# Variances of the decayed attention in the bank of its state products, and neighbourhood attention joined to the mixture of experts in one program region

## The chip, the cores and the metric

The kernel runs on one core of one Trainium2 chip. The metric is the device time of one execution in microseconds (us), the median of several runs. Engines: PE is TensorE (PEld its weight loads), ACT ScalarE, DVE VectorE, POOL GpSimd, SP the engine that issues most DMAs.

## The reference

A small language-model tower on 32 sequences of 512 tokens with 64 features: spectral token features, then two layers, each an attention and a feed-forward part, each of them preceded by a layer norm and followed by a residual sum.

```
x = tok(x)                                   # FFT features, MLP
x = x + neighbourhood_attn(layernorm(x))     # 8 heads, 31 neighbours, dilation 2
t = layernorm(x)
p = softmax(t @ router_w.T); top 2 of 8 experts, weights renormalised to sum 1
x = x + t + sum_e w_e * (gelu(t @ w1[e] + b1[e]) @ w2[e] + b2[e])
x = x + decayed_attn(layernorm(x))           # causal, scores scaled by 0.99^(q-k)
x = x + soft_moe(layernorm(x))               # routed softly by token position, 8 experts
```

Every layer norm needs, per token, 1/sqrt(variance + eps), spread over that token's 64 features.

## The kernel before

Activations stay in SBUF as 16 rows (`s.h`, `s.z`), each 128 partitions x 512 tokens, two sequences of 64 features one above the other. Each stage is one function that opens its own `nc.Block()`: a region in which every engine has its own hand-written instruction list, in order, joined to the others by semaphores alone. A region ends with a meeting of all engines. `unrolled(count, unroll, (lead, stage), ...)` writes the list of an engine: in loop step n it calls each stage for item n + lead, in the order in which the stages stand. So the order of an engine's queue is this list of stages, and a wait in it holds everything behind it on that engine.

**Layer norm.** When a row of `s.h` is final, POOL squares it (`square`, L488, into `s.sq[p % 8]`). For every four rows PE sums the squares over features into one PSUM bank (`variance`, L495), ACT takes Ln and Exp(-0.5 x) into `s.rstd`, SP writes that to DRAM (`hop`, L507) and reads it back spread over partitions (`spread`, L519, two DMAs per row), and POOL multiplies (`scaled`, L535). `keep_warm` (L502) issues bf16 products whose results nobody reads.

**Neighbourhood attention** (`neighbourhood_attention`, L902 to L1348). At its end PE makes the router's logits of the first four rows (L1153, L1160). DVE ranks them: nine instructions (`first_ranked`, L1309 to L1318) before the residual of the last row (L1295), and the rest (`next_ranked`, L1322 to L1341) after it. ACT gives the weights by an Exp of the gap (L1256) and computes the last norm (`deviations_of(LAST)`, L1244 and L1246) from the last variance, which PE makes between two groups of `keep_warm` (L1166 to L1168).

**Mixture of experts** (`mixture_of_experts`, L1387). 16 rows times 4 pairs of experts are 64 steps. Step n: PE `first(n)` (L1533, 4 products into two of three banks), ACT `gelu(n)` (L1604, two instructions), PE `expand(n)` (L1547, the route weights), DVE `weigh(n)` (L1735), PE `second(n)` (L1563). PE and ACT run `first` and `gelu` nine steps ahead of the loop up to step 42 (`AHEAD_G`, `LAST_AHEAD`), four ahead after it, `expand` and `weigh` three, `second` two. `first(n)` waits for the first half of `gelu(n-1)`. PE `turn` (L1523) turns the route weights and ACT copies them twice (L1618, L1622) before `expand(0)`. The router of the next four rows runs 24 steps ahead on PE, ACT and DVE. In step 33 ACT computes a norm with Ln and Exp (L1633, L1635). Between Gelu and these it loads other function tables. The region begins on ACT with a table load (L1582), and PE's first wait is for credits that ACT gives behind it.

**Decayed attention** (`decayed_attention`, L1760). Per row PE runs `scores` (L1886, then the state products L1892 into the bank `p_w`), `project` of the next row (L1871, L1876), and `outputs` (L1905, L1909, into the bank `p_y`). `project(n)` needs a copy of row n with its two halves exchanged, which SP fetches (`fetch_swapped`, L1355, two DMAs). SP's list per loop step n is `fetch(n+2)`, `former(n)` (the hop and spreads of the norm that feeds this stage) and `after(n)` (`normal(n-5)`, hop and spreads of the next norm). Variances go into `p_y`: `former` in step 0 and `after` in steps 5, 9 and 13 stand ahead of `outputs`, which waits until ACT has made the reciprocal deviations:

```
if at.n == 0:
    te.wait_ge(s.n_rstd, quad(2, LAST))
if at.n >= 5:
    te.wait_ge(s.n_rstd, quad(3, (at.n - 5) // 4))
unrolled(NP, 2, (0, scores), (1, project), (0, former), (0, after), (0, outputs))
```

Of the kernel before, what the change touches and what calls it, by code (L numbers as in the profile page):

```python
# [31 lines left out]
NP = NB // 2  # L32
# [869 lines left out]
def neighbourhood_attention(nc, s, v, r):  # L902

    with ExitStack() as ctx:
# [6 lines left out]
        def sem(name):  # L911
            return ctx.enter_context(nc.semaphore("na_" + name))
# [16 lines left out]
        logits_t = row(s.z, NP)  # L929
        logits, best, masked, picked, weights = [s.z[:, NP + 1 + k // 2, 256 * (k % 2):256 * (k % 2) + 256].rearrange("p (g e) -> p g e", e=NE) for k in range(5)]  # L930
        first_of, second_of, top, gap, w_best, w_next = [s.z[:, NP + 3, 256 + ROUTED * k:256 + ROUTED * k + ROUTED] for k in range(6)]
        p_route = p_s[1][:, 0].rearrange("p h a w -> p (h a w)")
        s_zero, s_rl, s_lt, s_rt, s_link, s_gap, s_less, s_next = [sem(x) for x in ("zero", "rl", "lt", "rt", "link", "gap", "less", "next")]
        p_first = p_t[:, 0:4, :].rearrange("p g c -> p (g c)")
        block = ctx.enter_context(nc.Block())

        @block.gpsimd
        def _(pool):
            nc.gpsimd.memset(r.ct_in[:], 0.0).then_inc(s_zero, 1)
# [76 lines left out]
        def _(te):  # L1016
# [139 lines left out]
            def first_logits_turned(at):  # L1156
                if at.n == TURNS - 1:
                    te.wait_ge(s_lt, 1)
                    for tile in range(4):
                        mm = nc.tensor.transpose(p_route[:, tile * 128:tile * 128 + 128], logits_t[:, tile * 128:tile * 128 + 128], const(s, "ident"))  # L1160
                    mm.then_inc(s_rt, 1)
# [4 lines left out]
            keep_warm(nc, s, p_o[:], 5)  # L1166
            variance_of(LAST)
            keep_warm(nc, s, p_o[:], 4)  # L1168

        @block.scalar  # L1170
        def _(sc):
# [64 lines left out]
            def fetch_first_logits(at):  # L1236
                if at.n == TURNS - 1:
                    sc.wait_ge(s_rl, 1)
                    nc.scalar.activation(logits_t, p_route, ACT.Copy).then_inc(s_lt, 1)
# [15 lines left out]
            sc.wait_ge(s_gap, 1)  # L1255
            nc.scalar.activation(gap, gap, ACT.Exp, scale=-1.0).then_inc(s_less, 1)  # L1256
            deviations_of(LAST)

        @block.vector
        def _(ve):  # L1260
# [37 lines left out]
            links = [0]  # L1298

            def linked(ins):  # L1300

                ins.then_inc(s_link, 1)
                links[0] += 1
                ve.wait_ge(s_link, links[0])

            def first_ranked():
                v = nc.vector
                ve.wait_ge(s_rt, 1)
                linked(v.tensor_copy(logits.rearrange("p (g b) e -> p g (b e)", b=2),  # L1309
                                     p_route.rearrange("p (g n) -> p g n", n=32)[:, :, 0:2 * NE]))  # L1310
                linked(v.tensor_reduce(first_of, logits, AX, ALU.max))
                linked(v.tensor_tensor(best, logits, over_experts(first_of), ALU.is_equal))
                linked(v.tensor_tensor(best, best, rank_of(s), ALU.mult))
                linked(v.tensor_reduce(top, best, AX, ALU.max))
                linked(v.tensor_tensor(best, best, over_experts(top), ALU.is_equal))
                linked(v.scalar_tensor_tensor(out=masked, in0=best, scalar=-3.0e38, in1=logits, op0=ALU.mult, op1=ALU.add))
                linked(v.tensor_reduce(second_of, masked, AX, ALU.max))
                v.tensor_tensor(gap, first_of, second_of, ALU.subtract).then_inc(s_gap, 1)  # L1318

            def next_ranked():  # L1320
                v = nc.vector
                linked(v.tensor_tensor(picked, masked, over_experts(second_of), ALU.is_equal))  # L1322
                linked(v.tensor_tensor(picked, picked, rank_of(s), ALU.mult))
                linked(v.tensor_reduce(top, picked, AX, ALU.max))
                linked(v.tensor_tensor(picked, picked, over_experts(top), ALU.is_equal))
                ve.wait_ge(s_less, 1)
                linked(v.tensor_scalar(top, gap, 1.0, None, ALU.add))
                linked(v.reciprocal(w_best, top))
                v.tensor_tensor(w_next, gap, w_best, ALU.mult).then_inc(s_next, 1)
                linked(v.tensor_tensor(best, best, over_experts(w_best), ALU.mult))  # L1330
                ve.wait_ge(s_next, 1)
                linked(v.tensor_tensor(picked, picked, over_experts(w_next), ALU.mult))
                linked(v.tensor_tensor(weights, best, picked, ALU.add))
                linked(v.tensor_copy(r.high[:], weights))
                ve.wait_ge(s_zero, 1)
                linked(v.tensor_tensor(weights, weights, r.high[:], ALU.subtract))
                v.tensor_copy(parts_of(r)[:, :, :, :, 0:NE], by_place(r.high[:]))
                linked(v.tensor_copy(r.middle[:], weights))
                v.tensor_copy(parts_of(r)[:, :, :, :, NE:2 * NE], by_place(r.middle[:]))
# [47 lines left out]
def mixture_of_experts(nc, s, r):  # L1387
# [3 lines left out]
    with ExitStack() as ctx:  # L1391
# [45 lines left out]
        def _(pool):  # L1437
# [919 lines left out]
```

## Time and profile before

| | before |
|---|---|
| median of 3 runs | 876.51 us (876.44 to 878.71) |
| profiled execution | 880.86 us, of it span 879.1 us |
| mean granted PE clock | 0.976 |
| busy PE | 804.4 us (92%) |
| busy DVE | 583.7 us (66%) |
| busy ACT | 476.7 us (54%) |
| busy POOL | 301.2 us (34%) |
| neighbourhood attention | to about 379 us |
| mixture of experts | 379 to 559 us |
| decayed attention | 559 to 671 us |

The sum of the engines' busy time is larger than the span because they work at once. Where PE is near its full share, a wait of another engine costs nothing; where PE waits, what it waits for sets the time.

### The profile page before, as it was taken

How to read it: one execution, taken by the hardware profiler on the slowest of the kernel's cores; microseconds unless marked ns; L12 is line 12 of the kernel's file. 1: busy time of each engine (PE TensorE's matmuls, PEld its weight loads, DVE VectorE, ACT ScalarE, POOL GpSimd, SP SyncE). 2: the span in 40 equal slices, each digit the busy share in tenths (PEclk: the TensorE clock that was granted, in tenths of full speed). 3: DMA queues.
4: the chain of work that ended last, by engine and by line, in shares of the span. 5: the costliest groups of instructions: out<-in, count | busy, mean ns of one | idle time of the engine just before them, and what ended most of it. 6: DMA issues, size and time to landing. Idle time of an engine off the chain costs nothing. (4 is left out here: it accounts for less than half of the span.)

```text
span 879.1 us, 28915 instructions
## 1 busy us (share of the span) xinstructions
PE 804.4 (92%) x12642; PEld 410.5 (47%) x12648; DVE 583.7 (66%) x854; ACT 476.7 (54%) x656; POOL 301.2 (34%) x292
## 2 busy tenths in 40 slices
PE   3989799999999999679999799799998899999996
PEld 2232377776776776413333233376663333333332
DVE  5547477777776776637777955477673377777776
ACT  2254377778778777346565656412221455555553
POOL 3235453633534423202443454473453710000000
PEclk9999799999999999979999999999999999999998
DMA  4210221002001001020000220053321011111111
GB/s 108 27 30 1 85 73 31 4 5 63 4 4 64 4 4 65 1 61 1 1 2 1 83 63 1 18 164 98 95 83 41 13 33 44 47 49 49 49 50 37
DMA packets 38670, 36.38 MB, mean 41 GB/s; under 512 B 20817, under 2 KB 25074, under 8 KB 38418
## 3 DMA queue, kind: packets, MB, share of 16 engines
q1 hardware_dynamic: 37474, 32.52, 13.1%
q8 instruction: 101, 1.65, 0.8%
q10 hardware_dynamic: 1072, 2.02, 0.7%
q14 instruction: 23, 0.19, 0.1%
HBM read 18.79 MB, written 7.34 MB: 30 GB/s over the span
## 5 line engine op out<-in xcount | busy, mean ns | idle before, releaser
L2233 ACT ACTIVATE se_a<-se_p,cols 128x512 f32<-128x512 f32 x128 | 92.8, 775 | 75.9 <-PE se_p L2186 75.9
L2253 DVE SCALAR_TENSOR_TENSOR se_a<-se_p,cols,z 128x1024 f32<-128x1024 f32 x64 | 82.2, 1284 | 48.8 <-PE se_p L2196 48.8
L1273 DVE TENSOR_REDUCE na_rowmax<-na_ps 128x16 f32<-128x1024 f32 x64 | 78.1, 1220 | 54.0 <-PE na_ps L1111 54.0
L1604 ACT ACTIVATE z<-me_p,cols 128x512 f32<-128x512 f32 x128 | 81.1, 685 | 59.4 <-PE me_p L1533 54.6
L1735 DVE TENSOR_TENSOR me_gw<-me_pc,z 128x1024 f32<-128x1024 f32 x64 | 78.3, 1223 | 46.7 <-PE me_pc L1547 38.3
L947 POOL TENSOR_TENSOR z<-na_k,const 128x512 f32<-128x512 f32 x62 | 62.5, 1040 | 129.6 <-ACT na_k L1192 129.6
L488 POOL TENSOR_TENSOR n_sq<-h 128x512 f32<-128x512 f32 x64 | 68.4, 1074 | 94.6 <-DVE h L858 40.0
L1563 PE MATMUL me_py<-me_gw,w_out 64*64 64x512 f32 x512 | 88.8, 601 | 0.0
L1533 PE MATMUL me_p<-z,moe_w 64*64 64x512 f32 x512 | 82.8, 621 | 6.4 <-issue 3.8
L535 POOL TENSOR_TENSOR z<-h,n_bc 128x512 f32<-128x512 f32 x58 | 75.1, 1306 | 25.7 <-DMA n_bc<-n_spread 25.6
L1276 DVE TENSOR_TENSOR z<-na_ps,na_rowmax 128x1024 f32<-128x1024 f32 x64 | 78.4, 1225 | 2.2
L1120 PE MATMUL na_pt<-const,z 128*128 128x128 f32 x512 | 70.0, 280 | 5.4 <-ACT z L1219 3.1
L1219 ACT ACTIVATE z<-z 128x1024 f32<-128x1024 f32 x64 | 67.4, 1053 | 8.1 <-DVE z L1276 7.4
L2186 PE MATMUL se_p<-z,f_w 64*64 64x512 f32 x512 | 68.8, 603 | 1.9 <-ACTq L548 1.1
L2196 PE MATMUL se_p<-se_a,f_w 64*64 64x512 f32 x512 | 68.3, 599 | 1.3 <-DVE se_a L2253 1.3
L1226 ACT ACTIVATE na_et<-na_pt 128x1024 f32<-128x1024 f32 x64 | 65.4, 1021 | 7.4 <-PE na_pt L1120 6.5
L2208 PE MATMUL se_py<-se_a,w_out 64*64 64x512 f32 x512 | 67.3, 589 | 0.5 <-DVE se_a L2253 0.5
L1120 PEld LDWEIGHTS na_pt<-const,z 128*128 128x128 f32 x512 | 56.7, 141 | 20.9 <-issue 15.3
L1454 POOL TENSOR_TENSOR h<-h,me_even 128x512 f32<-128x512 f32 x15 | 20.1, 1340 | 96.2 <-DVE me_even L1750 96.2
L1134 PEld LDWEIGHTS na_po<-na_v,na_et 128*32 128x32 f32 x4096 | 41.8, 110 | 21.8 <-ACT na_et L1226 11.4
L1111 PE MATMUL na_ps<-z,na_q 32*32 32x256 f32 x2048 | 51.6, 390 | 0.2
L1213 ACT ACTIVATE na_v<-na_pm 64x512 f32<-64x512 f32 x64 | 38.6, 602 | 21.3 <-PE na_pm L1066 20.9
(359 smaller groups left out, 1290.2 us busy)
## 6 DMA issues: line engine op xcount, KB each, us to landing
n_bc<-n_spread SPq DMA_DIRECT2D x116, 128.0 KB, 3.1
z<-z SPq DMA_DIRECT2D x64, 128.0 KB, 2.4
out<-se_rows SPq DMA_DIRECT2D x16, 256.0 KB, 2.1
n_spread<-n_rstd SPq DMA_DIRECT2D x12, 256.0 KB, 2.0
const<-in_const ACTq DMA_DIRECT2D x1, 1114.0 KB, 8.2
const<-in_const ACTq DMA_DIRECT2D x1, 562.0 KB, 4.2
f_w<-in_L_ffn_W SPq DMA_DIRECT2D x4, 128.0 KB
const<-in_const ACTq DMA_DIRECT2D x1, 258.0 KB, 3.0
```

The costliest lines, as they stand in the source:

```text
L488: return nc.gpsimd.tensor_tensor(s.sq[p % 8][:], row(s.h, p), row(s.h, p), ALU.mult)
L535: return eng.tensor_tensor(row(s.z, p), row(s.h, p), s.bc[p % 4][:], ALU.mult)
L1120: mm = nc.tensor.transpose(p_t[:, c, :], e[b][:, 2 * c:2 * c + 2, :].rearrange("p h w -> p (h w)"), const(s, "ident"))
L1273: nc.vector.tensor_reduce(rowmax[b][:], scored, AX, ALU.max).then_inc(s_max, 1)
L1276: nc.vector.tensor_tensor(e[b], scored, rowmax[b][:].unsqueeze(2).broadcast_to([128, GROUPS, WIN]), ALU.subtract).then_inc(s_diff, 1)
L1533: mm = nc.tensor.matmul(hidden(at.n, b)[half[e2], :], s.moe_w1[half[b], 2 * ep + e2, :], row(s.z, at.of(4))[half[b], :], start=True, stop= ...
L1563: mm = nc.tensor.matmul(p_y[half[b], e2, :], s.moe_w2[half[e2], ep, :], gw[at.k % 2][half[e2], b, :], start=(ep == 0 and b != e2), stop=(e ...
L1604: nc.scalar.activation(g[at.n % 7][:, b, :], hidden(at.n, b)[:], ACT.Gelu, bias=col(s, "moe_b1", ep)).then_inc(s_g, 1)
L1735: nc.vector.tensor_tensor(gw[at.k % 2][:], p_c[:], g[at.n % 7], ALU.mult).then_inc(s_gw, 1)
L2186: mm = nc.tensor.matmul(hidden(at.n, e2)[half[b], :], s.f1_w1[half[e2], 2 * ep + e2, :], z[half[e2], :], start=True, stop=True, skip_group ...
L2233: nc.scalar.activation(a1[at.k % 2][:, e2, :], hidden(at.n, e2)[:], ACT.Relu, scale=col(s, "f1_g1", 2 * ep + e2), bias=col(s, "f1_be1", 2 ...
L2253: nc.vector.scalar_tensor_tensor(out=a2[at.k % 2][:], in0=p_2[:], scalar=col(s, "f1_be2", ep), in1=s.f1_w[:, ep, :].unsqueeze(1).broadcast ...
```

## The change

Two parts. **One region:** attention and mixture share one block, so no meeting of the engines and no second block entry lies between them. Attention's tail loses the last variance, both groups of `keep_warm`, the last norm, and the ranking from its fifth instruction on. The ranking is completed at the head of DVE's mixture list (`rank_on`, 21 instructions), with Tanh instead of Exp for the weights; ACT does the Tanh behind `gelu(2)`. The last variance goes into a mixture bank behind `first(4)`, ACT copies it behind `gelu(4)`, and takes Ln and Exp at the end of step 8. `keep_warm` now has two products behind each of `first(0)` to `first(5)`. `gelu(6)` waits for the complete ranking, since its buffer holds the ranking's numbers. `turn(0)` and its two copies move one step back. POOL multiplies the last four rows by that norm in rows 2 and 3, two each, not one each in rows 0 to 3. **Decayed attention:** variances go into `p_w`, behind `outputs`; the next state products wait for ACT's Ln (`n_ln`), which has then read the bank.

```diff
@@ neighbourhood_attention
-            keep_warm(nc, s, p_o[:], 5)
-            variance_of(LAST)
-            keep_warm(nc, s, p_o[:], 4)
...
-            sc.wait_ge(s_gap, 1)
-            nc.scalar.activation(gap, gap, ACT.Exp, scale=-1.0).then_inc(s_less, 1)
-            deviations_of(LAST)
...
-            next_ranked()
@@ mixture_of_experts, POOL
-                if p < 4:
-                    rescale(1, 4 * LAST + p)
+                if 2 <= p < 4:
+                    rescale(1, 4 * LAST + 2 * (p - 2))
+                    rescale(1, 4 * LAST + 2 * (p - 2) + 1)
@@ mixture_of_experts, PE
                     if c == 1:
-                        te.wait_ge(s_route, linked_to(0, 1))
+                        te.wait_ge(r.s_h, done(NP - 1))
...
                 mm.then_inc(s_w1, 1)
-                if at.n < 2:
-                    keep_warm(nc, s, p_c[:, 0, :], 3)
+                if at.n < 6:
+                    keep_warm(nc, s, p_c[:, 1, :], 2)
+                if at.n == 4:
+                    te.wait_ge(s.n_sq, nth(1, NP - 1))
+                    variance(nc, s, LAST, p_y[:, 1, :]).then_inc(s.n_var, 1)
...
+                if at.n == 0:
+                    te.wait_ge(s_last, 1)
@@ mixture_of_experts, ACT
+                if at.n == 6:
+                    sc.wait_ge(s_ctin, done(0))
                 for b in range(2):
                     nc.scalar.activation(g[at.n % 7][:, b, :], hidden(at.n, b)[:], ACT.Gelu, bias=col(s, "moe_b1", ep)).then_inc(s_g, 1)
+                if at.n == 2:
+                    sc.wait_ge(s_gap, done(0))
+                    nc.scalar.activation(r.gap, r.gap, ACT.Tanh, scale=0.5).then_inc(s_tanh, 1)
+                if at.n == 4:
+                    sc.wait_ge(s.n_var, quad(1, LAST))
+                    nc.scalar.activation(s.rstd[:, LAST, :], p_y[:, 1, :], ACT.Copy).then_inc(s_last, 1)
+
+            def last_deviations(at):
+                if at.n == 8:
+                    sc.wait_ge(s_last, 1)
+                    nc.scalar.activation(s.rstd[:, LAST, :], s.rstd[:, LAST, :], ACT.Ln, bias=s.eps[:]).then_inc(s.n_ln, 1)
+                    sc.wait_ge(s.n_ln, 2 + LAST)
+                    nc.scalar.activation(s.rstd[:, LAST, :], s.rstd[:, LAST, :], ACT.Exp, scale=-0.5).then_inc(s.n_rstd, 1)
@@ decayed_attention, PE
+                if at.n == 1:
+                    te.wait_ge(s.n_ln, 7)
+                if at.n >= 6 and at.n % 4 == 2:
+                    te.wait_ge(s.n_ln, 8 + (at.n - 6) // 4)
...
-                if at.n == 0:
-                    te.wait_ge(s.n_rstd, quad(2, LAST))
-                if at.n >= 5:
-                    te.wait_ge(s.n_rstd, quad(3, (at.n - 5) // 4))
...
-                te.wait_ge(s_h, done(last))
+                te.wait_ge(s_st, done(last))
                 te.wait_ge(s.n_sq, nth(3, 4 * n + 3))
-                variance(nc, s, n, p_y).then_inc(s.n_var, 1)
+                variance(nc, s, n, p_w).then_inc(s.n_var, 1)
...
-            unrolled(NP, 2, (0, scores), (1, project), (0, former), (0, after), (0, outputs))
+            unrolled(NP, 2, (0, scores), (1, project), (0, outputs), (0, former), (0, after))
@@ build
-                neighbourhood_attention(nc, s, v, r)
-            mixture_of_experts(nc, s, r)
+                block = inner.enter_context(nc.Block())
+                neighbourhood_attention(nc, s, v, r, inner, block)
+            mixture_of_experts(nc, s, r, inner, block)
```

**ACT, steps 7 to 9 of the mixture.** Before: the copy of the router's logits (`me_logits_t`) stands between the Gelu pairs of `gelu(17)` and `gelu(18)`; `me_odd` is a copy of a finished row's sum.

```order
261 L1604 ACTIVATE z<-me_p,cols 128x512 x6
262 L1594 ACTIVATE me_logits_t<-me_pr 128x512
263 L1604 ACTIVATE z<-me_p,cols 128x512 x2
264 L1612 ACTIVATE me_odd<-me_py 128x512
265 L1604 ACTIVATE z<-me_p,cols 128x512 x4
```

The same place with the change:

```order
260 L1590 ACTIVATE z<-me_p,cols 128x512 x6
261 L1578 ACTIVATE me_logits_t<-me_pr 128x512
262 L1601 ACT_TABLE_LOAD
263 L1601 ACTIVATE n_rstd<-n_rstd,eps 128x512
264 L1603 ACT_TABLE_LOAD
265 L1603 ACTIVATE n_rstd<-n_rstd 128x512
266 L1590 ACT_TABLE_LOAD
267 L1590 ACTIVATE z<-me_p,cols 128x512 x2
268 L1611 ACTIVATE me_odd<-me_py 128x512
```

Three table loads, Ln and Exp now stand ahead of `gelu(18)`.

**PE, beginning of the decayed attention.** `da_pqk` and `da_pv` are `project`, `da_ps` and `da_pw` `scores`, `da_py` `outputs`, and L495 the variance. Before:

```order
603 L1886 MATMUL da_ps<-da_q,da_k 128x128 x8
604 L1892 MATMUL da_pw<-da_v,da_kd 64x64 x6
605 L1871 MATMUL da_pqk<-z,w_in 64x512 x4
606 L1876 MATMUL da_pv<-w_out,z 128x128 x8
607 L495 MATMUL da_py<-n_sq,const 32x512 x4
608 L1905 MATMUL da_py<-da_sm,da_v 64x128 x8
609 L1909 MATMUL da_py<-da_qd,da_state 128x128 x3
610 L1886 MATMUL da_ps<-da_q,da_k 128x128 x8
```

With the change:

```order
606 L1925 MATMUL da_ps<-da_q,da_k 128x128 x8
607 L1935 MATMUL da_pw<-da_v,da_kd 64x64 x6
608 L1910 MATMUL da_pqk<-z,w_in 64x512 x4
609 L1915 MATMUL da_pv<-w_out,z 128x128 x8
610 L1944 MATMUL da_py<-da_sm,da_v 64x128 x8
611 L1948 MATMUL da_py<-da_qd,da_state 128x128 x3
612 L495 MATMUL da_pw<-n_sq,const 32x512 x4
613 L1925 MATMUL da_ps<-da_q,da_k 128x128 x8
```

The variance moved behind both groups of `outputs` and into the bank `da_pw`; the steps 5, 9 and 13 change in the same way.

## Rows read from the trace of the kernel before

**Rows 1.** Windows: stretch, its us, busy us by engine, granted PE clock, DMA.

```profile
368.00:380.00 12.00, 5.43 (x18) 1.16 (x18) 10.28 (x24) 2.41 (x4) 3.37 (x3) 0.85 0.06 23
380.00:388.00 8.00, 7.60 (x34) 1.57 (x38) 0.00 (x0) 3.02 (x6) 1.26 (x1) 0.59 0.52 133
505.00:510.00 5.00, 4.48 (x32) 1.42 (x36) 2.63 (x6) 0.77 (x2) 0.00 (x0) 0.66 0.23 81
570.00:576.00 6.00, 5.65 (x58) 4.53 (x58) 1.69 (x2) 0.20 (x1) 0.27 (x1) 0.72 0.47 171
```

**Rows 2.** Timeline, attention to mixture: start, length, engine, line, work, idle before.

```profile
367.09 0.60 ACT L1234 ACTIVATE z<-na_pm 128x512 f32<-128x512 f32 x1 [3.58 <-PE na_pm L1078]
...
367.74 1.13 PE L1088 MATMUL na_pm<-z,w_out 128*128 128x512 f32 x2 [0.69 <-ACT z L1234]
...
371.06 0.74 DVE L1295 SCALAR_TENSOR_TENSOR h<-na_pm,cols,h 128x512 f32<-128x512 f32 x1
...
378.37 0.49 DVE L1341 TENSOR_TENSOR me_ctin<-z,me_middle 128x128 f32<-128x128 f32 x2
379.14 1.28 ACT L1582 ACT_TABLE_LOAD   x1 [2.70 <-PEq L904]
...
380.40 1.99 PE L1533 MATMUL me_p<-z,moe_w 64*64 64x512 f32 x8 [3.77 <-issue]
```

**Rows 3.** Timeline, opening of the mixture: `weigh(0)`.

```profile
396.80 1.23 DVE L1735 TENSOR_TENSOR me_gw<-me_pc,z 128x1024 f32<-128x1024 f32 x1 [5.03 <-PE me_pc L1547]
```

**Rows 4.** Timeline, DVE cast in step 8 and the product behind it.

```profile
421.09 1.35 DVE L1719 CAST me_ctin<-me_high 128x256 f32<-128x256 bf16 x1
...
423.83 0.41 PE L1547 MATMUL me_pc<-me_ct_parts,pick_b 64*64 64x512 bf16 x4 [1.89 <-DVE me_gw L1735]
```

**Rows 5.** Timeline, mixture steps 9 and 10: `gelu(18)` and `first(19)`.

```profile
427.18 1.27 ACT L1604 ACTIVATE z<-me_p,cols 128x512 f32<-128x512 f32 x2 [0.42 <-PE me_p L1533]
...
428.71 1.09 PE L1533 MATMUL me_p<-z,moe_w 64*64 64x512 f32 x8
```

**Rows 6.** Timeline of ACT, mixture step 33: loads, with the Ln of two tiles.

```profile
489.69 1.28 ACT L1633 ACT_TABLE_LOAD   x1
490.99 1.15 ACT L1633 ACTIVATE n_rstd<-n_rstd,eps 128x1024 f32<-128x1024 f32 x1
492.21 1.28 ACT L1635 ACT_TABLE_LOAD   x1
```

**Rows 7.** Timeline, PE behind a wait inside the mixture.

```profile
505.52 0.41 PE L1547 MATMUL me_pc<-me_ct_parts,pick_b 64*64 64x512 bf16 x4 [2.95 <-DVE me_gw L1735]
```

**Rows 8.** Waits, decayed attention: total us, times, longest.

```profile
PE da_py L1905 <- ACT n_rstd L1957: 4.7, 3, 1.6
...
PE da_py L1905 <- ACT n_rstd L1942: 2.7, 1, 2.7
```

**Rows 9.** Timeline, `fetch(3)` and `project(3)` of the decayed attention.

```profile
574.75 1.18 SPq L1355 DMA_DIRECT2D z<-z  x2
...
580.97 1.09 PE L1871 MATMUL da_pqk<-z,w_in 64*64 64x512 f32 x8
```

**Rows 10.** Swapped-row DMAs of 560 to 600 us, issue to landing.

```profile
DMA to landing us min/median/max: 2.2/2.6/3.6
```

**Rows 11.** Timeline, step 5 of the decayed attention up to `project(8)`.

```profile
600.99 0.69 ACT L1955 ACTIVATE n_rstd<-da_py,eps 128x512 f32<-128x512 f32 x1 [0.82 <-PE da_py L495]
601.71 0.63 ACT L1957 ACTIVATE n_rstd<-n_rstd 128x512 f32<-128x512 f32 x1
...
602.48 1.09 PE L1905 MATMUL da_py<-da_sm,da_v 128*64 128x128 f32 x16 [1.56 <-ACT n_rstd L1957]
603.50 0.94 PE L1909 MATMUL da_py<-da_qd,da_state 128*128 128x128 f32 x6
...
605.59 1.18 SPq L1355 DMA_DIRECT2D z<-z  x2
...
611.55 1.09 PE L1871 MATMUL da_pqk<-z,w_in 64*64 64x512 f32 x8
```

More of the change, by code:

```diff
@@ L928, in neighbourhood_attention @@
         s_first, s_near = sem("s_first"), sem("near")
[L929 to L933, printed above, removed]
+        p_route = p_s[1][:, 1].rearrange("p h a w -> p (h a w)")
+        s_rl, s_lt, s_rt = [sem(x) for x in ("rl", "lt", "rt")]
         p_first = p_t[:, 0:4, :].rearrange("p g c -> p (g c)")
-        block = ctx.enter_context(nc.Block())
+        r.s_h = s_h
         @block.gpsimd
         def _(pool):
-            nc.gpsimd.memset(r.ct_in[:], 0.0).then_inc(s_zero, 1)
+            nc.gpsimd.memset(r.ct_in[:], 0.0).then_inc(r.s_zero, 1)
             give_credits(pool, s_blk)
@@ L1317, in first_ranked @@
[L1317 to L1339, printed above, removed]
-                for b in range(2):
-                    v.tensor_tensor(parts_of(r)[:, :, b, :, 2 * NE:3 * NE], by_place(weights)[:, :, b], by_place(r.middle[:])[:, :, b], ALU.subtract)
@@ L1360, with route_buffers, chained, linked @@
 LINKS = 21
-def route_buffers(nc, ctx):
+def route_buffers(nc, s, ctx):
     r = Buffers()
     r.ct_in = ctx.enter_context(nc.sbuf_tensor("me_ctin", [128, 4, 2, 2, 2, ROUTES], F32))
+    r.logits_t = row(s.z, NB - 2)
+    r.logits, r.best, r.masked, r.picked, r.weights = [row(s.z, n)[:, c:c + 256].rearrange("p (g e) -> p g e", e=NE)
+                                                       for n, c in ((NB - 1, 0), (NB - 1, 256), (NB - 4, 0), (NB - 4, 256), (NB - 3, 0))]
+    r.first_of, r.second_of, r.top, r.gap, r.w_best, r.w_next = [row(s.z, NB - 3)[:, 256 + ROUTED * k:256 + ROUTED * k + ROUTED] for k in range(6)]
+    r.s_zero, r.s_link = [ctx.enter_context(nc.semaphore("r_" + x)) for x in ("zero", "link")]
+    r.links = 0
     r.high, r.middle = [ctx.enter_context(nc.sbuf_tensor("me_" + x, [128, ROUTED, NE], BF16)) for x in ("high", "middle")]
     return r
+def chained(ve, r):
+    def linked(ins):
+        ins.then_inc(r.s_link, 1)
+        r.links += 1
+        ve.wait_ge(r.s_link, r.links)
+    return linked
 def over_experts(x):
@@ L1576, in spreads @@
                     variance(nc, s, n, p_r).then_inc(s.n_var, 1)
-            unrolled(EP * NP, 16, (4, turn), (AHEAD_G, while_ahead(first)), (BEHIND_G, when_behind(first)), (3, expand), (2, second), (AHEAD, logits_of), (0, spreads))
+            unrolled(EP * NP, 16, (4, turn), (AHEAD_G, while_ahead(first)), (BEHIND_G, when_behind(first)), (3, first_turn), (3, expand), (2, second), (AHEAD, logits_of), (0, spreads))
         @block.scalar
@@ L1583, in _ @@
             give_credits(sc, s_ct, s_parts, s_g, s_copied, s_odd)
-            for x in (s_lt, s_tanh):
-                sc.sem_inc(x, done(0))
+            give_credits(sc, s_tanh)
+            sc.sem_inc(s_lt, done(0))
             def router(at):
@@ L1635, in deviations @@
                         nc.scalar.activation(s.rstd[:, 0:2, :], s.rstd[:, 0:2, :], ACT.Exp, scale=-0.5).then_inc(s.n_rstd, 2)
-            unrolled(EP * NP, 16, (4, fetch), (AHEAD_G, while_ahead(gelu)), (BEHIND_G, when_behind(gelu)), (2, fetch_odd), (4, fetch_whole), (AHEAD, router), (0, deviations))
+            unrolled(EP * NP, 16, (4, fetch), (AHEAD_G, while_ahead(gelu)), (BEHIND_G, when_behind(gelu)), (3, first_fetch), (2, fetch_odd), (4, fetch_whole), (AHEAD, router),
+                     (0, deviations), (0, last_deviations))
         @block.vector
@@ L1954, in deviations @@
                 sc.wait_ge(s.n_z, nth(2, NP - 1))
[L1955 removed]
+                nc.scalar.activation(s.rstd[:, n, :], p_w[:], ACT.Ln, bias=s.eps[:]).then_inc(s.n_ln, 1)
                 sc.wait_ge(s.n_ln, 8 + n)
```

126 lines of the change are left out of this document (79 added, 47 removed).

## The prediction

> **What bounds the kernel now.** I read the busy shares first: PE is busy 92% of the span, so only what delays PE counts. The windows come next, because they show the few places where PE does not run full [rows 1]. From 368 to 380 us PE is busy 5.4 of 12 us while DVE is busy 10.3: the ranking of the first four rows bounds the end of the attention. From 380 to 388 us PE is granted 0.59 of full speed, a mixture of the levels 1.2 and 2.4 GHz, which costs 8 x 0.41 = 3.3 us. The timeline then names the steps between the regions [rows 2]: ACT's last attention copy ends at 367.69, PE's at 368.87, DVE's ranking at 378.86; the table load starts 0.28 later and PE's first mixture product at 380.40, as that load ends. In the decayed attention the waits show PE standing for the reciprocal deviations, once 2.7 us and three times together 4.7 us [rows 8].
>
> **Term 1, one region.** Nothing now holds ACT behind DVE. It can branch and load its table 0.28 us behind its last copy: 367.97 to 369.25. `first(0)` starts at 369.2, 11.2 us earlier than 380.40. The steps up to `first(6)` go at the pace of `first` (1.09), half a Gelu pair (0.64) and two hand-overs of 0.1, so 1.9 us [rows 5]; six of them are 11.4 us. Router logits, their transposes and the moved variance do not quite fit in the gaps; I charge 1.8. `first(6)` starts at 382.4. Its 1.1, the Gelu pair 1.3, the first route copy 0.6 (as the 0.60 of rows 2), `expand(0)` 0.4 [rows 4] and hand-overs 0.2 bring `weigh(0)` to 386.0, where it was 396.80 [rows 3]: **-10.8 us**. In this the slow-clock loss of 3.3 us is gone, because PE no longer stands from 376 to 380 us, and the turn and copy that used to be early now stand on the path.
>
> Is DVE in time? Before, 17 instructions took 371.80 to 378.86, 0.42 us each [rows 2]. Five fewer stand ahead of the last residual, so it moves from 371.06 to about 369.0 and ends at 369.8. Nine instructions lead to the Tanh wait, reached at 373.5. Tanh comes behind `gelu(2)`, which ends near 376.3. Twelve instructions more end at 381.7. `gelu(6)` wants them at 383.6, so 1.9 us of cover remain.
>
> The two removed groups of `keep_warm`, the removed variance and ACT's Exp of the gap were beside DVE's chain and count nothing by themselves. The new `keep_warm` pairs stand in the gap in which PE waits for Gelu and are covered too. The squares and the hop come later than before, but the four rows scaled by them are first needed by the router in step 24, more than 30 us behind step 8.
>
> **Term 2, POOL.** In step 8 a DVE cast takes 1.35 us beside a POOL product, and PE waits 1.89 us [rows 4]. POOL's scaling in row 1 is moved away. Bounds: 0 if the square still collides, -1.35 at most. I take **-1.0**, since the POOL row that leaves is the one beside the cast.
>
> **Term 3, table loads inside the mixture.** ACT now executes, between `gelu(17)` and `gelu(18)`, three loads, an Ln and an Exp. Durations: 1.28 each [rows 6], Ln 0.69 and Exp 0.63 of one tile [rows 11]; with gaps of 0.02 to 0.07 [rows 6] this is 5.2 us. ACT was idle 0.42 there [rows 5], so `gelu(18)` is 4.8 us late. Being nine steps ahead does not help: `first(19)` waits for its first half and stands on PE in front of `expand(13)` and `second(12)`. First half done at 427.18 + 4.8 + 0.64 = 432.6, `first(19)` at 432.8 where it was 428.71: 4.1 us. Behind a wait of 2.95 us [rows 7] PE ran at 0.66 from 505 to 510 us [rows 1], which costs 5 x 0.34 = 1.7 us; this wait is longer, so I add it. **+5.8 us**, and PE has no slack afterwards to take it back.
>
> Here the Trainium skill has two rules. ScalarE: Activation LUTs (What ACT_TABLE_LOAD costs) puts every switch at 1.28 us plus a drain of about 1.38 us. In rows 6 the load is followed by its function in 0.02 us and preceded by 0.07 us, so the trace does not show the drain; with it the term would be about 4.1 us larger. The same page (Table sets) says that Ln followed by Exp needs one load, as one set holds both. The trace shows a load ahead of each [rows 6], and the change's list for ACT has the same; with one load fewer the term would be 1.3 us smaller. I go by the rows.
>
> **Term 4, start of the decayed attention.** `outputs(0)` now goes ahead of the variance: 1.09 + 0.94 = 2.0 us [rows 11], less 0.1 for overlap, so the variance, the deviations, the hop and all that SP has behind them come 1.9 us later. PE itself saves the 2.7 us wait. But SP's `fetch(3)` stands behind the hop. It was issued at 574.75, its second half 0.6 later [rows 9], and lands 2.6 us behind that [rows 10], at 577.9; now at 579.8. `project(3)` was at 580.97 [rows 9] and cannot start before 579.8: -1.1 us. Without that limit it would be wanted at about 577.2, so PE stands about 2.6 us. The same stand before led to a clock of 0.72 from 570 to 576 us [rows 1], 6 x 0.28 = 1.7 us. That loss lay ahead of 580.97 and is in the old time; now it would come again behind it. **+0.6 us** with it, -1.1 without. The new wait for `n_ln` before the state products costs 0.3 us here, inside PE's slack against SP.
>
> **Term 5, steps 5, 9 and 13.** Each loses its wait, 4.7 us together [rows 8]. ACT's Ln (0.69) now runs beside `scores`, which is longer, so the new wait is hidden. What is late next is SP again: variance 1.95 us later, so `fetch(8)`, issued at 605.59 [rows 11], lands at 605.59 + 0.6 + 2.6 + 1.95 = 610.7, while `project(8)`, at 611.55 before, is wanted 1.56 earlier, at 610.0. That gives 0.7 us back in step 5 and in step 9; behind step 13 no row is fetched. Bounds: -4.7 with nothing given back, 0 if the DMAs take everything. **-3.3 us.**
>
> **Sum.** -10.8 - 1.0 + 5.8 + 0.6 - 3.3 = -8.7 us. Against the profiled execution of 880.86 us (span 879.1 and 1.76 around it) this is 872.2. The median of the runs is 876.51, 4.35 below the profiled one; with the same difference I predict **867.8 us**.
>
> **Rivals.**
> - *The clock holds* through the waits of terms 3 and 4. For it: behind the 1.56 us wait of step 5 PE ran at once at its full pace, 1.09 us for L1905 [rows 11]. Against: the windows behind the 2.95 us and the 2.7 us wait [rows 1], which these waits equal or exceed. -8.7 - 3.4 = -12.1: 864.4 us. Chance 0.17.
> - *The opening runs at half speed* as it did from 380 to 388, since PE is lightly used before it. Against: it is no longer empty for 4 us. Up to 3.3 us come back: 871.1 us. Chance 0.12.
> - *The ranking is late.* POOL and DVE collide as in rows 4, the cover of 1.9 us is used up, and `gelu(6)` waits. The point: DVE instructions at 0.6 us each in place of 0.42. At 0.9 us it costs 4 us: 871.8 us. Chance 0.06. The change would then not do what it says, as the ranking still bounds the opening.
> - *One load fewer*, the rule of the page named above: 1.3 us less, 866.5 us. Both lists speak against it. Chance 0.02.
> - *The drain of 1.4 us per switch*, the page's other rule: 871.9 us. Chance 0.02.
> - *Slower: the fetches of swapped rows become the bound.* SP issues them behind a hop that is now 1.95 us later, in steps 0, 5 and 9, among the spreads' traffic. If each lands x later than 2.6 us, and each stall slows the clock (1.7 more in steps 5 and 9), the price is 3x + 3.4. It cancels the gain at x = 1.8, a landing of 4.4 us; at x = 3 the time is 867.8 + 12.4 = 880.2 us. Against: the slowest landing was 3.6 us [rows 10]. Chance 0.05.
>
> **The numbers.** The forecast has the remaining 0.56. The low end takes the held clock and half of what term 5 gives back; the high end takes the slow opening or the drain and a term 5 near zero: 862.0 to 873.5 us. A change of 0.3% (2.6 us) is about what a measurement of this kernel can tell from none. Only the last rival, and half a dozen small misses together, come near it: faster 0.92, same 0.04, slower 0.04.
>
> **What would show it.** In the new trace: PE's first mixture product within 0.5 us of the end of ACT's load near 369 us; `weigh(0)` near 386; three table loads behind the router's logits copy of step 8 with a PE wait near 4 us and a clock below 1; PE waiting for a swapped row before `project(3)`; 0.5 to 1 us before `project(8)` and `project(12)`; no PE wait for the reciprocal deviations. The forecast is wrong if the opening does not start before 371 us, or if the wait in step 10 is below 2 us.

## The result

The change runs at 873.0 us (median of 20 runs, 867.88 to 878.58), the kernel before at 877.02 us (median of 20, 872.83 to 879.55). The ratio is 0.9956, 95% interval 0.9938 to 0.9973: faster by 4.0 us, where 8.7 were forecast. The profiled execution of the change took 872.89 us (span 871.2, mean granted clock 0.980) against 880.86 for the kernel before (0.976). This one pair says -8.0 us, close to the forecast; the runs say half of it. What follows looks for the 4.7 us between the forecast and the runs.

First the handover from attention to mixture, in the timeline of the change:

```profile
366.37 0.60 ACT L1228 ACTIVATE z<-na_pm 128x512 f32<-128x512 f32 x1 [3.68 <-PE na_pm L1075]
366.99 1.28 ACT L1566 ACT_TABLE_LOAD   x1
...
367.02 1.12 PE L1085 MATMUL na_pm<-z,w_out 128*128 128x512 f32 x2 [0.69 <-ACT z L1228]
368.08 1.09 PE L1512 MATMUL me_p<-z,moe_w 64*64 64x512 f32 x8
...
378.51 0.49 DVE L1681 TENSOR_TENSOR me_ctin<-z,me_middle 128x128 f32<-128x128 f32 x2
...
384.35 1.23 DVE L1773 TENSOR_TENSOR me_gw<-me_pc,z 128x1024 f32<-128x1024 f32 x1 [2.95 <-PE me_pc L1529]
```

Against [rows 2, 3] the load directly follows ACT's last copy, and `first(0)` starts 1.06 us behind the start of PE's last attention product where it was 12.66. It starts as that product ends, 0.19 us before ACT's load does, so the load is not on PE's path here. It runs at full pace: 1.09 us, where it took 1.99. DVE's ranking (to 379.00) is no longer ahead of anything: `gelu(6)`, the first to want its result, starts at 382.02. From that last product (L1085, L1088 before) to `weigh(0)` it is 17.33 us, before 29.06.

Step 8 of the mixture, ACT and then PE:

```profile
413.17 1.28 ACT L1601 ACT_TABLE_LOAD   x1
414.46 0.72 ACT L1601 ACTIVATE n_rstd<-n_rstd,eps 128x512 f32<-128x512 f32 x1
415.20 1.28 ACT L1603 ACT_TABLE_LOAD   x1
416.50 0.63 ACT L1603 ACTIVATE n_rstd<-n_rstd 128x512 f32<-128x512 f32 x1
417.14 1.28 ACT L1590 ACT_TABLE_LOAD   x1
...
419.18 1.99 PE L1512 MATMUL me_p<-z,moe_w 64*64 64x512 f32 x8 [4.01 <-ACT z L1590]
```

The three loads are there, each followed by its function in 0.01 or 0.02 us, and `first(19)` waits 4.01 us and then takes 1.99 instead of 1.09 us. A little earlier stands the cast of [rows 4], now with no POOL product beside it:

```profile
408.55 0.28 DVE L1757 CAST me_ctin<-me_high 128x256 f32<-128x256 bf16 x1
...
410.22 0.41 PE L1529 MATMUL me_pc<-me_ct_parts,pick_b 64*64 64x512 bf16 x4 [0.81 <-DVE me_gw L1773]
```

The cast takes 0.28 us where it took 1.35, and PE waits 0.81 where it waited 1.89.

The decayed attention, from the waits of TensorE there, and the timeline of its swapped rows:

```profile
PE da_pqk L1910 <- DMA z<-z: 6.0, 3, 3.3
...
PE da_pw L1935 <- ACT n_rstd L1980: 0.4, 1, 0.4
```

```profile
567.22 3.10 SPq L519 DMA_DIRECT2D n_bc<-n_spread  x4
570.42 1.18 SPq L1310 DMA_DIRECT2D z<-z  x2
...
573.66 1.67 PE L1910 MATMUL da_pqk<-z,w_in 64*64 64x512 f32 x8 [3.35 <-DMA z<-z]
...
600.52 1.97 SPq L519 DMA_DIRECT2D n_bc<-n_spread  x2
602.59 1.18 SPq L1310 DMA_DIRECT2D z<-z  x2
...
605.96 1.09 PE L1910 MATMUL da_pqk<-z,w_in 64*64 64x512 f32 x8 [1.72 <-DMA z<-z]
...
630.33 1.09 PE L1910 MATMUL da_pqk<-z,w_in 64*64 64x512 f32 x8 [0.94 <-DMA z<-z]
```

The 7.4 us of waits for the reciprocal deviations [rows 8] are gone. In their place stand 6.0 us of waits for swapped rows (`project(3)`, `project(8)`, `project(12)`) and 0.4 for `n_ln`. One kind of wait was exchanged for another. The spreads (L519) that SP issues ahead of these fetches also take longer to issue than in the kernel before, where they are

```profile
572.26 2.39 SPq L519 DMA_DIRECT2D n_bc<-n_spread  x4
...
604.38 1.11 SPq L519 DMA_DIRECT2D n_bc<-n_spread  x2
```

### The profile page after: what moved, and what is told of

Its sections match the earlier page's. It is cut to its first block and busy times, and to the rows that moved or that the text cites. A ratio compares the mean times of both kernels' runs of the same rounds, so it can differ in the third digit from the quotient of the medians.

```text
span 871.2 us, 28909 instructions
## 1 busy us (share of the span) xinstructions
PE 799.5 (92%) x12638; PEld 408.3 (47%) x12645; DVE 584.0 (67%) x853; ACT 480.8 (55%) x660; POOL 301.2 (35%) x292
## 5 line engine op out<-in xcount | busy, mean ns | idle before, releaser
L1590 ACT ACTIVATE z<-me_p,cols 128x512 f32<-128x512 f32 x128 | 81.1, 685 | 59.1 <-PE me_p L1512 54.3
L1117 PEld LDWEIGHTS na_pt<-const,z 128*128 128x128 f32 x512 | 56.4, 141 | 20.8 <-issue 15.3
```

Of the source, the lines that this page charges most:

```text
L1117: mm = nc.tensor.transpose(p_t[:, c, :], e[b][:, 2 * c:2 * c + 2, :].rearrange("p h w -> p (h w)"), const(s, "ident"))
L1590: nc.scalar.activation(g[at.n % 7][:, b, :], hidden(at.n, b)[:], ACT.Gelu, bias=col(s, "moe_b1", ep)).then_inc(s_g, 1)
```

## The experiments

Two pieces of the change were run alone, then two of its suspected costs were taken away.

**The region alone.** The change with the decayed attention of before:

```diff
-            unrolled(NP, 2, (0, scores), (1, project), (0, outputs), (0, former), (0, after))
+            unrolled(NP, 2, (0, scores), (1, project), (0, former), (0, after), (0, outputs))
...
-                variance(nc, s, n, p_w).then_inc(s.n_var, 1)
+                variance(nc, s, n, p_y).then_inc(s.n_var, 1)
```

> The change with the decayed attention of before: one program region, the variance of the last four rows behind first(4), the ranking in the mixture, and nothing else. Theory (profiles read event by event): the pair of profiles gave first(0) 12.3 us earlier, the pair in step 8 another 1.15, the three table loads +6.4, so that the decayed attention starts 6.9 us earlier; the decayed part's own net was -1 us. So the profiled execution of this kernel should start its decayed attention near 553.4 us and end 1 us later than that of the change, and its median should lie 1 us above the change's 873.0, near 874, ratio to before near 0.9965. Rival (the decayed part is the whole of the gain that the medians show, the region gives back in clock and loads what it saves): ratio 1.000, median near 877.

Measured: 874.53 us, ratio 0.9972 (0.9948 to 0.9996). Its decayed attention started at 555.00 us, not near 553.4, and its profiled execution ended 1.6 us above that of the change instead of 1. The median came where the first theory had it, and the rival's 1.000 lies just outside the interval: the region is most of the gain.

**The decayed attention alone.** The kernel before with the change's variances, the same edit in the other direction.

> The kernel before with the decayed attention of the change: variances in the bank of the states' products, behind the outputs. The two program regions stay. Theory: the outputs no longer wait for the deviations (4.7 us at three steps before), but the fetch of the swapped row stands behind the later hop, and project(3), project(8), project(12) wait for it by 3.35, 1.72 and 0.94 us (a sum of 6.0) as in the change: net -1 us, median near 876, ratio 0.9985 to 1.000. Rival (all of the gain of the medians comes from here): ratio 0.9956, median near 873. Rival (the waits for the fetch cost more where the clock falls): ratio 1.002.

Measured: 879.17 us, ratio 1.0028 (1.0005 to 1.0051): no gain, rather a loss. The waits are as expected, 5.4 us for swapped rows in place of 7.4 for the deviations:

```profile
PE da_pqk L1871 <- DMA z<-z: 5.4, 3, 3.5
```

The rival in which the decayed attention is the gain is out, and so is the theory's 0.9985 to 1.000; nearest is the rival with 1.002, the waits for the fetch costing more where the clock falls. But by its profile the part itself is not longer (109.6 us, table below). What is longer is the span behind the first product of the last mixture: 192.6 us against 190.9 in that of the kernel before, with the clock at 0.92 and 0.90 from 700 to 720 us. The table comes back to this.

**No table loads in step 8.** This kernel leaves out the deviation of the last four rows.

```diff
-                    nc.scalar.activation(s.rstd[:, LAST, :], s.rstd[:, LAST, :], ACT.Ln, bias=s.eps[:]).then_inc(s.n_ln, 1)
+                    nc.scalar.activation(s.rstd[:, LAST, :], s.rstd[:, LAST, :], ACT.Copy).then_inc(s.n_ln, 1)
...
-                    nc.scalar.activation(s.rstd[:, LAST, :], s.rstd[:, LAST, :], ACT.Exp, scale=-0.5).then_inc(s.n_rstd, 1)
+                    nc.scalar.activation(s.rstd[:, LAST, :], s.rstd[:, LAST, :], ACT.Copy).then_inc(s.n_rstd, 1)
```

> The change with Ln and Exp of the last four rows' deviations replaced by two ACT.Copy on the same data, so no table load stands between expand(16) and gelu(18); it leaves out the deviation of the last four rows (its output is not the reference's there). Theory: first(19) no longer waits 4.0 us for gelu(18) and the clock of the stretch behind it stays up (together 6.4 us in the pair of profiles): median near 866.6 to 868, ratio to before 0.989. Rival (the loads fall into a stretch that is limited elsewhere, PE makes the time up before the next wait): median within 1.5 us of the change's 873. Rival (clock alone: the wait goes, the clock falls elsewhere in the mixture): -4.0, near 869.

Measured: 865.08 us, ratio 0.9874 (0.9842 to 0.9907), a little past the theory's 866.6 to 868; both rivals are out. Waits for the Gelu (L1590) fall from 4.8 to 0.8 us, and the clock of 410 to 430 us is whole again. Windows of the change, then of this kernel (the figure ahead of the DMA share is the granted clock):

```profile
410.00:430.00 20.00, 15.77 (x124) 5.43 (x128) 9.06 (x14) 13.70 (x19) 6.21 (x6) 0.83 0.22 66
```

```profile
410.00:430.00 20.00, 19.41 (x182) 6.88 (x180) 17.00 (x23) 13.23 (x23) 12.71 (x10) 1.00 0.20 68
```

**The fetch one step earlier.** The change with another lead for SP's swapped rows:

```diff
-            unrolled(NP, 2, (2, fetch), (0, former), (0, after))
+            unrolled(NP, 2, (3, fetch), (0, former), (0, after))
```

> The change with SP fetching the swapped row three steps ahead instead of two (its due time 3 in SP's table), so that fetch(3), fetch(8) and fetch(12) are issued before the hop of the deviations and not behind it. Theory: the waits of project(3), project(8), project(12) for the swapped row (3.35 + 1.72 + 0.94 = 6.0 us) go, and with them the clock fall at 572 to 578 us (1.2 of 2.1 us); what is left is what the former row allows, which is ready about one step (5 us) before. Median 6 to 7 us below the change, near 866.5, ratio to before 0.988. Rival (the slot of three steps ahead is still being read, or the fetch waits for the former row, so SP stands there and the hop behind it comes late): gain under 1.5 us, with waits for the deviations in their place. Rival (only the first wait matters): -3.4, near 869.6.

Measured: 870.45 us, ratio 0.9926 (0.9897 to 0.9955), 2.5 below the change where 6 to 7 were expected. All three waits for swapped rows went, but none of the stated theories had what came instead, at `outputs(2)`:

```profile
574.36 1.04 POOL L488 TENSOR_TENSOR n_sq<-h 128x512 f32<-128x512 f32 x1
575.35 0.86 POOL L1871 TENSOR_TENSOR da_qd<-da_q,const 128x384 f32<-128x384 f32 x1
...
576.36 0.91 PE L1948 MATMUL da_py<-da_qd,da_state 128*128 128x128 f32 x6 [2.82 <-POOL da_qd L1871]
```

POOL's decayed queries stand behind its rescaling of rows 8 and 9, which waits for the same late spread as the fetch did. Two queues, SP's and POOL's, were held by one hop, and PE met the first that it needed. In the profile the part is 3.4 us shorter than in the change: 6.0 us of waits less these 2.8 are most of it. By the medians alone the gain is not clear, since the two intervals overlap.

**The kernel before, twice more,** to see what belongs to the code and what to one execution.

> The kernel before, unchanged, profiled once more, for its granted clock by stretch. Theory (the clock falls of the first profile were those of one execution): the clock of 380 to 388 us is 1.00, or another stretch has fallen in its place; the waits of TensorE are the same ones to 0.1 us; the time is nearer 877 than 880.86, and the difference to 880.86 is what the clock lost less (18.8 us of full clock were missing in the first profile, read by stretches of 10 us). Rival (the falls belong to the code of that stretch, so term 1 of the prediction was right in full): the same two falls at 368 to 388 us, a time near 880.

> The same kernel again, a third execution with its profile. Theory: the TensorE waits agree again; the stretches of lower clock differ from those of the other two executions in one or more places, and the time follows their sum with 0.6 to 0.8 us per 0.001 of mean clock (the slope over the runs of the kernel before and of the change so far). Rival: the same stretches in all three.

Measured: 879.28 and 877.03 us. The waits for deviations agree (4.7 and 2.7 us in all three). The main claim of the first theory fell, and its rival held: the low clock at the handover is in both profiles again:

```profile
370.00:390.00 20.00, 12.29 (x66) 2.83 (x64) 9.88 (x25) 7.22 (x11) 3.84 (x3) 0.74 0.21 67
```

```profile
370.00:390.00 20.00, 13.21 (x72) 3.06 (x73) 8.77 (x23) 8.30 (x13) 3.83 (x3) 0.74 0.21 67
```

The first profile of the change has there

```profile
370.00:390.00 20.00, 17.49 (x137) 5.29 (x138) 13.97 (x30) 12.92 (x22) 1.68 (x2) 1.00 0.00 1
```

So term 1's clock gain was real. In part the theory holds: the first execution also had the clock down at 360 to 370 us (0.87) and at 660 to 670 us (0.83), where the other two have 1.00, and they have falls of their own. Summed over the whole windows of 10 us, 18.8, 18.7 and 15.3 us of full clock are missing. This does not give the times: the second execution is 1.6 us shorter than the first with 0.1 us less missing, and the third 2.3 us shorter than the second with 3.4 less.

**The change once more.**

> The change, unchanged, profiled once more, for the lengths of its parts between fixed events. By the profiles so far (from the last output product of the first attention to weigh(0): 27.95 to 29.06 us in four profiles with the program of before, 17.33 in six with that of the change; from weigh(0) to the first product of the decayed attention: 163.1 to 163.5 against 169.0 to 170.1 with three loads; decayed attention up to the soft router 109.6 to 111.0 against 109.8 to 110.3) theory: 17.3, 169 to 170.1, 109.8 to 110.3 again, total to the soft router about 5 us less than before, not 8. Rival (the first pair's decayed attention, 0.75 us shorter than before's, is the rule): 109.4 or less.

Measured: 875.37 us; the parts are 17.36, 171.93 and 110.27 us. The mixture is longer than I allowed (clock 0.83 in 380 to 390 us besides the fall behind the loads); the rival is out. Over all profiles the lengths between fixed events are (us; the events are the starts of the last output product of the first attention, of `weigh(0)`, of the first product of the decayed attention and of the first product of the soft router, and the end of the span):

| program | handover, opening | mixture | decayed attention | rest |
|---|---|---|---|---|
| before, first profile | 29.06 | 163.52 | 111.04 | 207.74 |
| before, second | 27.95 | 163.13 | 110.12 | 207.79 |
| before, third | 28.05 | 163.28 | 110.18 | 207.74 |
| before + new decayed attention | 28.96 | 163.51 | 109.61 | 209.49 |
| region alone | 17.33 | 170.07 | 110.26 | 207.64 |
| the change, first | 17.33 | 169.04 | 110.29 | 207.52 |
| the change, second | 17.36 | 171.93 | 110.27 | 209.44 |
| no loads | 17.33 | 162.94 | 109.84 | 209.32 |
| one table set (below) | 17.33 | 166.70 | 109.83 | 207.60 |
| fetch early | 17.33 | 169.68 | 106.92 | 209.30 |
| fetch and queries early (below) | 17.32 | 169.18 | 101.57 | 207.75 |
| all of it (below) | 17.33 | 166.90 | 102.52 | 209.23 |

Means over the profiles that share a part, without the rest: handover 28.51 to 17.33, -11.2; mixture with three loads (five profiles) 169.98 against 163.36, +6.6; decayed attention, new against old (five and four), 109.97 against 110.40, -0.4. Together -5.0 us, inside the interval of the ratio (-5.4 to -2.4). The first pair, by the same columns, gives -11.7, +5.5 and -0.7, so -7.0, and the other 0.9 us of the span came from code that the change does not touch (the last product of the attention was 0.7 us earlier, the rest of the span 0.2 shorter).

The rest has the same code in all twelve and two lengths. With the old order of the decayed attention it is 207.6 to 207.8 us (four of four), with the new one 207.5 to 207.8 in three and 209.2 to 209.5 in five. In those five, and in none of the others, the clock falls some 36 us behind the first product of the soft router, where PE has just waited 1.8 to 1.9 us for DVE. The change itself has it both ways, first and second profile:

```profile
700.00:710.00 10.00, 9.92 (x92) 3.88 (x96) 7.60 (x13) 5.30 (x8) 0.00 (x0) 1.00 0.19 54
```

```profile
700.00:710.00 10.00, 9.33 (x72) 3.49 (x76) 6.21 (x10) 3.62 (x6) 0.07 (x1) 0.83 0.18 52
```

The wait does not settle it: the region alone, the first profile of the change and two more have it without the fall. Whether the new order makes this fall likelier or chance did, twelve profiles do not show. Over the change's two profiles it takes 0.7 us back from the 5.0.

**Two loads in place of three.** The change with one line more ahead of the Ln of step 8:

```diff
+                    sc.preload_act_table_set("natural_log_exp_and_others")
```

> The change with the set natural_log_exp_and_others preloaded ahead of the Ln of the last four rows in step 8, so that Ln and Exp share one load and gelu(18) takes a second one: two loads in place of three. Theory (each load delays gelu(18), for which first(19) waits, one for one): first(19) waits 4.0 - 1.28 = 2.7 us, median 1.3 us below the change's 873.0, down to 2 us with a clock that falls less: 871 to 871.7, ratio to before 0.994. Rival (a clock fall is set off by the wait whatever its length, so a shorter wait gives back its length only or nothing): within 1 us of 873. Rival (below some length the clock does not fall): near 869.

Measured: 871.71 us, ratio 0.9939 (0.9913 to 0.9965), as the theory had it, though this interval overlaps with the change's and does not exclude the rival near 873. What decides is the profile. In its timeline the Exp follows the Ln without a load and `first(19)` waits 1.28 us less:

```profile
413.89 1.28 ACT L1601 ACT_TABLE_LOAD   x1
415.19 0.72 ACT L1602 ACTIVATE n_rstd<-n_rstd,eps 128x512 f32<-128x512 f32 x1
415.94 0.63 ACT L1604 ACTIVATE n_rstd<-n_rstd 128x512 f32<-128x512 f32 x1
416.59 1.28 ACT L1590 ACT_TABLE_LOAD   x1
...
418.63 1.99 PE L1512 MATMUL me_p<-z,moe_w 64*64 64x512 f32 x8 [2.73 <-ACT z L1590]
```

```profile
410.00:430.00 20.00, 16.46 (x140) 5.75 (x140) 11.68 (x16) 13.65 (x21) 6.70 (x6) 0.91 0.20 66
```

Clock missing in these 20 us: 3.4 in all five profiles with three loads, 1.8 here, none without loads. The median moved by 1.3 only, less than the interval is wide; the mixture in the profile is 2.3 us shorter than in the first profile of the change, and that is more than the 1.28 of the wait. So the shorter wait also gave clock back, against the rival.

**Queries early too.** The kernel with the early fetch, and POOL's list changed:

```diff
-            unrolled(NP, 2, (1, decayed_queries), (0, former), (0, after))
+            def queries_ahead(at):
+                if 2 <= at.n < 6:
+                    decayed_queries(at)
+
+            def queries_behind(at):
+                if not 2 <= at.n < 6:
+                    decayed_queries(at)
+
+            unrolled(NP, 2, (1, queries_behind), (2, queries_ahead), (0, former), (0, after))
```

> The change with the fetch three steps ahead, as run before (median 870.45), and with POOL's decayed queries of steps 2 to 5 a step earlier, ahead of the rescaling of the rows 8 and up that waits for the spread deviations. In the run with the early fetch alone, outputs(2) waited 2.82 us for these queries, which stood behind that rescaling, right where the wait for the fetch had been. Theory: this wait goes too (at most 1 us of it is left at outputs(3)), with the clock fall behind it: median 3 to 4.5 us below 870.45, near 867, ratio to before 0.9885. Rival (the next wait behind it takes most of it, for the spread of rows 8 to 11 or for the swapped row): median within 1 us of 870.45.

Measured: 864.76 us, ratio 0.9853 (0.982 to 0.9887), 5.7 below the early fetch alone and 8.2 below the change, more than expected; the rival is out. The waits of TensorE in the decayed attention that are left there are the opening, the last variance and small ones:

```profile
PE da_pw L495 <- POOL n_sq L488: 2.0, 1, 2.0
PE da_pqk L1918 <- ACT L1980: 1.7, 1, 1.7
...
PE da_py L1952 <- DVE da_sm L2033: 0.8, 1, 0.8
PE da_pw L1943 <- ACT n_rstd L1988: 0.4, 1, 0.4
```

and the clock is 1.00 from 550 to 670 us. The part is 8.7 us shorter than in the change: 6.0 us are the waits, and the other 2.7 come with two falls of the clock that the change has there (1.7 us of full clock each). The early fetch and queries were not run with the old order of the variances, whose 7.4 us of waits for the deviations stand ahead of `outputs` whatever is fetched.

**All of it.** Fetch and queries early, and the set loaded once for Ln and Exp at both places in the mixture (the second is that of [rows 6]):

> The change with everything that gained: the fetch three steps ahead, the decayed queries of steps 2 to 5 a step earlier, and one table set for Ln and Exp at both places in the mixture (two loads in place of three, twice). Theory: the run with fetch and queries early had 864.76; one load fewer in step 8 was worth 2.3 to 3.4 us of the mixture's length in a profile and 1.3 in the median; the second place (before first(35) or so) starts from a wait of about the same kind, so another 1.3 to 2.5: median 860 to 862.5, ratio to before 0.980 to 0.9825. Rival (the loads in the second place are hidden or its wait is set by something else): 863 to 863.5. Rival (clock falls move elsewhere): 864.

Measured: 863.82 us (858.6 to 865.28), ratio 0.9833 (0.9796 to 0.9869), the lowest median: 9.2 us below the change, 13 below the kernel before; its interval overlaps with that of the run before it. The time lies between the two rivals, and the profile has something of both. As the first has it, the mixture is no shorter than with one place mended (166.90 and 166.70 us). As the second has it, the clock falls at 640 to 660 us and at 690 to 700 us (0.83), where the run before it has 1.00 at the same places of the program; the decayed attention is 0.95 us longer and the rest 1.5, which takes back what the mixture gained. At the second place PE still waits 2.95 us for DVE behind the loads, as in [rows 7]; the saved load only turned a wait of 1.08 us for the route copy into one of 0.71 for DVE:

```profile
485.83 0.41 PE L1529 MATMUL me_pc<-me_ct_parts,pick_b 64*64 64x512 bf16 x4 [0.71 <-DVE me_gw L1775]
...
496.25 0.64 PE L1529 MATMUL me_pc<-me_ct_parts,pick_b 64*64 64x512 bf16 x4 [2.95 <-DVE me_gw L1775]
```

## Why the prediction was wrong

The mechanisms were the right ones, and the one pair of profiles nearly bore the sum out. The size that the runs show is half of it, for two steps that were mis-sized by about 2 us each: the slow clock behind the table loads in term 3, and in terms 4 and 5 what SP's later fetches take back.

- **Term 1 (-10.8).** Right: -11.7 in the pair, -11.2 over the profiles, with the clock gain in it. PE's first product came 0.19 us before the load ended, directly behind its own last attention product and not behind the load as forecast; DVE's ranking had 3 us of cover where 1.9 were forecast.
- **Term 2 (-1.0).** Right: the wait shrank by 1.08 us.
- **Term 3 (+5.8).** This step failed by its clock. The wait was right (4.01 us; 4.1 forecast), the clock behind it was not: 3.4 us of full clock are missing, in each of the five profiles with three loads, where I charged 1.7 from the stretch behind a 2.95 us wait [rows 1, 7]. Terms 2 and 3 together were to cost 4.8 and cost 6.6 over the profiles (5.5 in the pair). Without loads the mixture is 7.0 us shorter, 4.0 of it the wait. The drain of 1.38 us per switch that the Trainium skill states (ScalarE: Activation LUTs, What ACT_TABLE_LOAD costs) does not show: the third load here starts 0.01 us behind the Exp and the Gelu 0.02 behind the load, and leaving out one load shortened the wait by 1.28 us and no more. The same page of the Trainium skill says that one set holds Ln and Exp (Table sets), and this is right once the program asks for that set, as the run with one set shows; left to itself this program takes two loads.
- **Term 4 (+0.6).** The Ln came 1.9 us later as forecast, but `fetch(3)` was issued 7.70 us behind it where it was 6.99, since the four spreads between them took 3.10 us to issue instead of 2.39. So `project(3)` waited 3.35 us (2.6 forecast) and came 20.27 us behind the first product of the part where it was 20.65: 0.4 us gained and not 1.1. The slow clock stood behind it as forecast (1.67 us for a product of 1.09). At `project(4)` the account is +1.2.
- **Term 5 (-3.3).** This is the second step that failed. Taken from one product to the next (`project(4)`, `project(8)`, `project(12)`, the last variance), steps 5, 9 and 13 gave +0.15, -0.62 and -1.63, so -2.1 in the pair. "What is late next is SP again" named the right transfer, but I took SP's delay as the 1.95 us of the moved outputs. `fetch(8)` was issued 5.46 us behind the start of the Ln where it was 4.60 before [rows 11], since the two spreads ahead of it took 1.97 us to issue instead of 1.11. This belongs to the new order: the spreads of step 0 take 2.39 us in all four profiles with the old one and 2.85 to 3.33 in all eight with the new one, those of step 5 1.11 against 1.47 to 2.10; in step 9 they are alike (1.10 to 1.19). Why they take longer was not tested. And a second fall of the clock goes with the new order: seven of its eight profiles show one between 640 and 680 us (0.91 over 650 to 670 us in both of the change), of the four with the old order only the first does. Terms 4 and 5 together: -2.7 forecast, -0.4 found over the profiles (-0.7 in the pair).
- **The step to the median.** "With the same difference" carried the whole change of one profiled execution over to the runs. But that execution lay 3.8 us above the median of 20, with one fall of the clock inside the decayed attention that the other two lack (111.04 us against 110.12 and 110.18). A fall that the next execution lacks is no part of what a change can save. It is one fall, though, and the terms above carry most of the miss. The profiled times of the kernel before are 880.86, 879.28 and 877.03 (mean 879.1), of the change 872.89 and 875.37 (mean 874.1): -4.9.
- **The rivals.** The clock did not hold, the opening ran at full speed (17.32 to 17.36 us in all eight profiles with the region), the ranking was in time, and no drain appeared. The slower side came in its mild form: the fetches did become the bound, but landed as before (3.2 to 3.5 us from issue to product; 0.6 + 2.6 before), so they took back what the change had saved there and no more.
- **The range.** 862.0 to 873.5 us does not follow from its own words. The held clock (864.4) and half of what term 5 gives back (0.7) make 863.7, and the slow opening or the drain (871.1 or 871.9) with 3.3 us for term 5 make 874.4 or 875.2. The 873.0 measured lies inside either way; the size of the gain is what was missed.

Open stays why the new decayed attention alone, in the program of before, measures 2 us slower while its part is not longer; its one profile has 1.75 us of that in the rest, with the clock fall there. The same fall, in one of the change's two profiles, would be 0.7 of the 1 us between -5.0 by parts and -4.0 by medians; that difference is within the interval as well. That the new order brings it is not shown.

## What to carry to other kernels

When a wait is moved off the path, list every queue behind the event that is now later: here one hop held SP's fetches and POOL's queries, and only with both moved ahead of it did the reordering clearly pay (-8.2 us beside the change's own 4.0). Put a switch of activation table where no one waits for the engine, and ask for a set that holds both functions; three loads cost 7 us where PE waited for them, of which the waiting was 4, and one load fewer gave nothing where DVE held PE. Before summing against one profile, take two or three of the same kernel and compare them by parts: what differs between them is not yours to save.

## What the hardware showed

- The granted clock falls in pieces. Read by windows of 10 us, a fall takes about 1.7 us of full clock (0.83 in one window, or shared by two), or a multiple: 3.4 behind the three loads, 1.8 behind two. The totals per execution, over whole windows of 10 us, run from 10.2 to 20.6 us in the twelve profiles.
- A wait of the same length need not bring a fall. In the soft mixture PE waits 1.8 to 1.9 us for DVE in nine of the twelve profiles; behind it the clock falls in five (and the rest of the span is about 1.7 us longer) and stays at 1.00 in four.
- Falls behind the long waits (370 to 390 us before, 410 to 430 with the loads) came in every profile of the same code. Others came and went at the same place with the same code: 90 to 120 us lost 5.1 us in one profile of the kernel before and 6.8 in the next, and 690 to 700 us was at 0.83, 0.89 and 1.00 in its three.
- Over 23 runs of the kernel before, the time went with the mean granted clock: 872.56 us at 0.984, 876.86 at 0.980, 879.11 at 0.974. This spread of 7 us is larger than what the change gives.
- Each load of an activation table took 1.28 us in every profile; where ACT had no wait beside it, it started 0.01 to 0.08 us behind the instruction before it and the next followed in 0.01 or 0.02 us.
